# Dense stage between attention layers of a graph network, moved chunk by chunk into the attention pass

## What is computed

```python
def _gat_layer(x, src, dst, W, a_src, a_dst, b):
    h = (x @ W.T).reshape(N, H, C)
    alpha_s = jnp.einsum('nhc,hc->nh', h, a_src)
    alpha_d = jnp.einsum('nhc,hc->nh', h, a_dst)
    e = _leaky_relu(alpha_s[src] + alpha_d[dst])
    e_max = jax.ops.segment_max(e, dst, num_segments=N)
    e_exp = jnp.exp(e - e_max[dst])
    denom = jax.ops.segment_sum(e_exp, dst, num_segments=N)
    alpha = e_exp / denom[dst]
    msg = alpha[:, :, None] * h[src]
    out = jax.ops.segment_sum(msg, dst, num_segments=N)
    return out.reshape(N, H * C) + b
...
x = jax.nn.relu(_gat_layer(x, src, dst, W1, as1, ad1, b1))
x = jax.nn.relu(_gat_layer(x, src, dst, W3, as3, ad3, b3))
return _gat_layer(x, src, dst, W2, as2, ad2, b2)
```

## Time and profile before

| | us |
|---|---|
| median of 3 runs | 11625.31 (11618.93 to 11647.12) |
| the profiled execution | 11634.58 |
| its span | 11632.5 |
| attention passes: first gather, last gather starts | 5139.9, 11494.5 |
| first dense stage between passes (reciprocals from) | 7210.2 |
| second dense stage between passes (reciprocals from) | 9369.2 |

### The profile page before, as it was taken

The page is one execution under the profiler, slowest core; times in us unless marked ns, Lnnn a source line. Parts: engine busy times, 40 slices in busy tenths (PEclk is TensorE's granted clock), DMA queues, the critical chain, the costliest instruction groups (busy, mean ns, idle before and its releaser), DMA issues. The chain is left out here.

```text
span 11632.5 us, 269882 instructions
## 1 busy us (share of the span) xinstructions
PE 8371.0 (72%) x95122; PEld 6886.6 (59%) x95123; DVE 7236.0 (62%) x21427; ACT 2833.5 (24%) x9590; POOL 8097.8 (70%) x8039
## 2 busy tenths in 40 slices
PE   4878888889999799956666667566666666666665
PEld 3777777768778687835555555455555545555553
DVE  5777777779999654565555556555555565555556
ACT  2444333434444455520000001100000020000001
POOL 5777777737577475727777775677777757777774
PEclk9898888979999898955555555555555555555555
DMA  4666666649899686812222221222222212222221
GB/s 133 189 188 190 188 178 182 187 127 258 222 257 258 193 267 210 254 25 43 43 43 43 43 43 33 43 43 43 43 43 43 43 33 43 43 43 43 43 43 28
DMA packets 1192998, 1285.98 MB, mean 111 GB/s; under 512 B 234298, under 2 KB 1039893, under 8 KB 1191410
## 3 DMA queue, kind: packets, MB, share of 16 engines
q1 hardware_dynamic: 629602, 628.36, 17.7%
q0 software_dynamic: 254464, 283.59, 12.8%
q10 hardware_dynamic: 307600, 356.66, 10.6%
HBM read 982.93 MB, written 284.81 MB: 109 GB/s over the span
## 5 line engine op out<-in xcount | busy, mean ns | idle before, releaser
L2285 POOL DMA_INDIRECT rows<-gat_table,wgt x2457 | 2353.5, 958 | 962.2 <-issue 747.9
L2285 POOL DMA_INDIRECT Y<-gat_table,wgt x2394 | 2293.6, 958 | 729.6 <-issue 729.6
L2466 DVE TENSOR_TENSOR rep<-rep,layers 128x560 f32<-128x560 f32 x693 | 514.9, 743 | 2372.6 <-ACT rep L2399 2372.6
L1001 POOL DMA_INDIRECT bins<-scratch,slots x1288 | 1373.2, 1066 | 500.0 <-issue 384.9
L2311 PE MATMUL bank<-rep,work 128*32 128x80 f32 x11088 | 527.7, 341 | 1495.5 <-DVE rep L2466 1495.5
L2311 PEld LDWEIGHTS bank<-rep,work 128*32 128x32 f32 x11088 | 324.0, 158 | 1836.6 <-DVE rep L2466 1836.6
L2358 PE MATMUL bank<-work,msg 128*72 128x32 f32 x9702 | 1308.7, 309 | 0.0
L2358 PEld LDWEIGHTS bank<-work,msg 128*72 128x72 f32 x9702 | 1215.8, 237 | 44.5
L1191 DVE TENSOR_TENSOR xT<-counts,xT 112x480 f32<-112x480 f32 x1716 | 1114.5, 650 | 80.0 <-issue 48.3
L1069 PE MATMUL bank<-xT 112*64 112x120 f32 (+1 forms) x13728 | 1138.5, 277 | 26.4 <-ACT xT L1379 24.4
L2345 PE MATMUL bank<-scratch,work 128*128 128x64 f32 x2772 | 754.8, 426 | 515.5 <-DVE scratch L2436 515.5
(11 more groups left out here) (277 smaller groups left out, 16940.1 us busy)
## 6 DMA issues: line engine op xcount, KB each, us to landing
xT<-bins ACTq DMA_DIRECT2D x1716, 119.0 KB
work<-adj SPq DMA_DIRECT2D x184, 780.0 KB
work<-near_table SPq DMA_DIRECT2D x1118, 128.0 KB
near_table<-work SPq DMA_DIRECT2D x598, 128.0 KB
xT<-near_table SPq DMA_DIRECT2D x598, 128.0 KB
adj<-work ACTq DMA_DIRECT2D x299, 240.0 KB
bins<-zeros ACTq DMA_DIRECT2D x46, 1547.0 KB, 9.6
work<-in_attr SPq DMA_DIRECT2D x231, 224.0 KB
```

The costliest lines, as they stand in the source:

```text
L1001: nc.gpsimd.indirect_dma_start(bins, bass.IndirectOffsetOnAxis(slots[b % RANK_LEAD][:, r * G + j:r * G + j + 1], 0), binf[r][:, j, :], Non ...
L2285: nc.gpsimd.indirect_dma_start(rows[g % GR][:, j, :], None, gat_table, bass.IndirectOffsetOnAxis(edge_sources[:, g * G + j:g * G + j + 1], ...
```

## The change

The dense stages behind the first and the second pass go; their steps become part of `gat_pass`. Chunk c is due when turn `EARLY[c]` + 7 has added the last group that can reach its columns, by the mean number of edges of a node and two groups to spare (21, 40, 59 and so on; the last two are 229 and 231). Its steps then follow one to a turn, in eight turns: denominators on PE, reciprocal and product on DVE, activation on ACT, forward on PE, copies on DVE and ACT, the store on SP. One chunk has one set of banks (0, 1 and 2) and of buffers. A chunk is now 512 adjacent columns. Rows go to a second table, since the pass still gathers from the first; the tables take turns. DVE, not POOL, sets the denominators' rows back to 1. The set-up finds, for each chunk, the lowest destination of all groups from `EARLY[c]` on; where one still points into the chunk, `widest` is raised, and the fallback, which has a dense stage of its own, takes over. (Its part of the diff is left out.)

```diff
@@ -52,6 +52,8 @@
+MARGIN = 2
+EARLY = [-(-CH * (c + 1) * E // (N * GE)) + MARGIN for c in range(NCH - 1)] + [NG]
@@ -131,7 +133,7 @@
-        gat_table = dram("gat_table", (NP, ROW))
+        gat_tables = [dram(f"gat_table{i}", (NP, ROW)) for i in range(2)]
@@ -408,6 +410,13 @@
+                lowest_left, late = [qbuf[:].rearrange("p t d -> p (t d)")[:, NG + i * (NCH - 1):NG + (i + 1) * (NCH - 1)] for i in range(2)]
+                for c in range(NCH - 1):
+                    link(nc.vector.tensor_reduce(lowest_left[:, c:c + 1], first[:, EARLY[c]:], AX, ALU.min))
+                link(nc.vector.scalar_tensor_tensor(late, counts[:, 1:NCH], float(CH), lowest_left, ALU.mult, ALU.is_gt))
+                link(nc.vector.tensor_reduce(bad[:, 1:2], late, AX, ALU.max))
+                link(nc.vector.tensor_scalar(bad[:, 1:2], bad[:, 1:2], float(WIN), None, ALU.mult))
+                link(nc.vector.tensor_tensor(widest[:], widest[:], bad[:, 1:2], ALU.max))
@@ -2246,12 +2310,20 @@
-        def gat_pass(name):
+        def gat_pass(k, nxt, gat_table, next_table):
...
+            DELAY = 7
+            STEPS = 8
+            bias = col["gb" + k]
+            def chunk_at(n, step):
+                c = EARLY.index(n - DELAY - step) if n - DELAY - step in EARLY else None
+                return c if nxt else None
@@ -2272,8 +2344,17 @@
-                    for g in range(NG):
-                        body(g)
+                    def keep(c):
+                        sp.wait_ge(q["gtile_ready"].handle, q["gtile_ready"].at(c + 1))
+                        sp.dma_start(next_table[columns(c), :].rearrange("(p t) d -> p t d", t=TC), gbuf).then_inc(s_gtab[0].handle, 16)
+                    for n in range(NG + DELAY + STEPS + 2):
+                        if real(n):
+                            body(n)
+                        if chunk_at(n, STEPS) is not None:
+                            keep(chunk_at(n, STEPS))
+                    if nxt:
+                        sp.wait_ge(s_gtab[0].handle, s_gtab[0].at(16 * NCH))
@@ -2358,6 +2439,25 @@
+                    def denominators(c):
+                        pe.wait_ge(q["acc_done"].handle, q["acc_done"].at(EARLY[c]))
+                        if due(c):
+                            pe.wait_ge(q["inverted"].handle, q["inverted"].at(c))
+                        nc.tensor.matmul(bank[0][LO, :], denom[:], accT[0:ROW, columns(c)], start=True, stop=True).then_inc(q["prod_ready"].handle, 1)
+                    def forward(c):
+                        pe.wait_ge(q["x_ready"].handle, q["x_ready"].at(c + 1))
+                        if due(c):
+                            pe.wait_ge(q["gtile_ready"].handle, q["gtile_ready"].at(c))
+                            pe.wait_ge(q["kept"].handle, q["kept"].at(c))
+                        nc.tensor.matmul(bank[1][0:D + 40, :], attend[nxt][:], x_of, start=True, stop=True)
+                        for t in range(TC):
+                            last = nc.tensor.matmul(bank[2][:, t * ROW:(t + 1) * ROW], x_of.rearrange("r (p t) -> r t p", t=TC)[:, t, :],
+                                                    attend[nxt][:, 0:ROW], start=True, stop=True)
+                        last.then_inc(q["nodes_ready"].handle, 1)
@@ -2370,9 +2470,13 @@
+                        if chunk_at(n, 4) is not None:
+                            forward(chunk_at(n, 4))
+                        if chunk_at(n, 0) is not None:
+                            denominators(chunk_at(n, 0))
...
-                    for n in range(NG + 6):
+                    for n in range(NG + DELAY + STEPS):
@@ -2400,6 +2504,19 @@
+                    def activate(c):
+                        ac.wait_ge(q["mean_ready"].handle, q["mean_ready"].at(c + 1))
+                        if due(c):
+                            ac.wait_ge(q["nodes_ready"].handle, q["nodes_ready"].at(c))
+                        nc.scalar.activation(x_of, mean_of, ACT.Relu, bias=bias).then_inc(q["x_ready"].handle, 1)
+                    def keep_scores(c):
+                        ac.wait_ge(q["nodes_ready"].handle, q["nodes_ready"].at(c + 1))
+                        nc.scalar.activation(xT[0:H, columns(c)], bank[1][D:D + H, :], ACT.Copy)
+                        nc.scalar.activation(auxT[0:H, columns(c)], bank[1][D + 32:D + 32 + H, :], ACT.Copy).then_inc(q["kept"].handle, 1)
@@ -2407,8 +2524,12 @@
-                    for n in range(NG + 5):
+                        if chunk_at(n, 5) is not None:
+                            keep_scores(chunk_at(n, 5))
+                        if chunk_at(n, 3) is not None:
+                            activate(chunk_at(n, 3))
+                    for n in range(NG + DELAY + STEPS):
@@ -2520,7 +2641,28 @@
-                    DELAY = 7
+                    def invert(c):
+                        ve.wait_ge(q["prod_ready"].handle, q["prod_ready"].at(c + 1))
+                        if due(c):
+                            ve.wait_ge(q["mean_ready"].handle, q["mean_ready"].at(c))
+                        nc.vector.reciprocal(inverse_of, bank[0][LO, :]).then_inc(q["inverted"].handle, 1)
+                    def mean(c):
+                        ve.wait_ge(q["inverted"].handle, q["inverted"].at(c + 1))
+                        if due(c):
+                            ve.wait_ge(q["x_ready"].handle, q["x_ready"].at(c))
+                        nc.vector.tensor_tensor(mean_of, inverse_of, accT[LO, columns(c)], ALU.mult).then_inc(q["mean_ready"].handle, 1)
+                        nc.vector.memset(accT[D:ROW, columns(c)], 1.0).then_inc(q["cleared"].handle, 1)
+                    def take(c):
+                        ve.wait_ge(q["nodes_ready"].handle, q["nodes_ready"].at(c + 1))
+                        if due(c):
+                            ve.wait_ge(s_gtab[0].handle, s_gtab[0].at(16 * c))
+                        nc.vector.tensor_copy(accT[LO, columns(c)], bank[1][LO, :])
+                        nc.vector.tensor_copy(gbuf, by_tile(bank[2], ROW)).then_inc(q["gtile_ready"].handle, 1)
@@ -2540,6 +2682,12 @@
+                        if chunk_at(n, 5) is not None:
+                            take(chunk_at(n, 5))
+                        if chunk_at(n, 2) is not None:
+                            mean(chunk_at(n, 2))
+                        if chunk_at(n, 1) is not None:
+                            invert(chunk_at(n, 1))
@@ -2562,7 +2710,11 @@
-            gat_further(name)
+            if nxt:
+                s_gtab[0].done(16 * NCH)
+                for n in ["prod_ready", "inverted", "mean_ready", "cleared", "x_ready", "nodes_ready", "kept", "gtile_ready"]:
+                    q[n].done(NCH)
+            gat_further(k, nxt, gat_table, next_table)
@@ -2574,11 +2726,9 @@
-        gat_pass("gat0")
-        gat_dense("1", "3")
-        gat_pass("gat1")
-        gat_dense("3", "2")
-        gat_pass("gat2")
+        gat_pass("1", "3", *gat_tables)
+        gat_pass("3", "2", *gat_tables[::-1])
+        gat_pass("2", None, gat_tables[0], None)
```

More of the change, by code:

```diff
@@ L530, in further @@
                             closing(g)
+                if ending is not None:
+                    ending()
                 engine.nop()
@@ L628, in _, with gat_further @@
                     further(ve, group, window, closing, NG, cleared)
-        def gat_further(name):
+        mean_of, inverse_of, x_of = [scratch[0:D, i * CH:(i + 1) * CH] for i in range(3)]
+        columns = lambda c: slice(c * CH, (c + 1) * CH)
+        def gat_further(k, nxt, gat_table, next_table):
+            ending = lambda body: body if nxt else None
             with nc.Block() as block:
@@ L646, in group, with dense @@
                                      ).then_inc(f_load.handle, 16)
-                    further(sp, group, whole=NG, opening=restored)
+                    def dense():
+                        for c in range(NCH):
+                            sp.wait_ge(f_restored.handle, NCH + 2 + c)
+                            sp.dma_start(next_table[columns(c), :].rearrange("(p t) d -> p t d", t=TC), gbufs[0]).then_inc(f_load.handle, 16)
+                        sp.wait_ge(f_load.handle, 16 * (2 * NCH + 2 * NG))
+                    further(sp, group, whole=NG, opening=restored, ending=ending(dense))
                 @block.gpsimd
@@ L697, in window, with dense @@
                         last.then_inc(token_tensor_vector.handle, 1)
-                    further(pe, group, window, whole=NG, opening=restored)
+                    further(pe, group, window, whole=NG, opening=restored, ending=ending(dense))
                 @block.scalar
                 def _(ac):
+                    def dense():
+                        for c in range(NCH):
+                            ac.wait_ge(token_vector_scalar.handle, 1)
+                            ac.sem_clear(token_vector_scalar.handle)
+                            nc.scalar.activation(x_of, mean_of, ACT.Relu, bias=col["gb" + k]).then_inc(token_scalar_tensor.handle, 1)
                     def group(g, base=0.0):
```

(2 more changed lines are left out.)

42 lines of the change are left out of this document (36 added, 6 removed).

## The result

The changed kernel takes **11532.94 us** (median of 4 runs, 11528.61 to 11535.81) against 11629.9 for the kernel before (4 runs, 11618.93 to 11647.12): a ratio of 0.9915, with an interval of 0.9898 to 0.9932. It is 0.85% faster, with an interval that leaves 1 out. It lies inside the stated range, outside the 11488 to 11522 that the forecast itself was given, and 33 us above the 11500 forecast. The two profiled executions have spans of 11532.9 and 11632.5, so 99.6 us went where 125.6 were forecast.

The account below looks back on a forecast made before the run. POOL's gathers and their issue were taken to bound the passes. Boundaries -132, set-up +4.4 and gathers beside DVE +2 summed to -125.6 us: 11509 from the profiled 11634.6, or 11500 against the runs' median; range 11484 to 11535.

Parts of the forecast that it names:

- What bounds the kernel: Attention passes: POOL's seven gathers and their issue, 8.83 us a group; at each pass boundary POOL gathers nothing for 89 us.
- the first rival: Pass boundaries: chunks 11 and 12 run one behind the other at strided prices, 37 us a boundary, 11528 us; chance 0.07.
- The chain behind T0: Pass boundary: steps of chunks 11 and 12 from the last add's end to the next first gather, 23 us for 89.
- its strided rival: Dense steps of a chunk: DVE's product or copy at the price with a stride, 1.22 us, against 0.62 over adjacent columns.
- The check block that now stands here as well: ... 1.5: Pass boundary: the check block takes 1.9 us as before, less what is counted already, so it adds 1.5 us.
- Set-up +4.4: Set-up: 12 more reductions and four small operations on DVE's chain add 4.4 us (3 to 6).
- One body in nineteen runs some 2 us late. That delays no gather: First two passes: PE's chunk work exceeds one body's slack; gathers have about 53 us before POOL would wait.
- I take +2 us, because the 0.94 row is nearest in kind: First two passes: gathers beside a busier DVE cost 2 us in all, between bounds of nothing and 63 us.
- 14 us from the chunks' own products: First two passes: by the skill's rule alone, each chunk's 0.62 us product is lost 22 times; about 11512 us.
- The other rivals: Passes: DVE stretches gathers (0.06), DVE shuts POOL out (0.06), or each pass goes through the fallback, over 17,600 us (0.01).
- gathers stretched by every added instruction: First two passes: each of 110 added DVE instructions lengthens a gather by 0.57 us, 63 us in all, 11561 us; chance 0.06.
- POOL shut out: First two passes: POOL stands during every added DVE instruction and following gathers stretch, 186 us, about 11684 us; chance 0.06.

Follow-up runs that it names:

- the short-fallback run: The changed kernel with the fallback's own dense stage left out, nothing else; 11521.61 us.
- the added product: The kernel before, with one more DVE product of 64 x 512 in each turn, both inputs in SBUF, result not used; 11756.35 us.
- the copy: The kernel before, with one more DVE copy of 64 x 512 from PSUM in each turn, result not used; 11745.34 us.
- the six-chunk fallback: The changed kernel with the fallback's dense stage written out for 6 chunks in place of 13; 11529.22 us.

## Why the prediction was right, and where it was off

- **The range: right in part by luck.** What bounds the kernel, and what the change wins, were right. But the forecast's own band, 11488 to 11522, was missed; the range reached to 11535 to take in the first rival, whose time (11528) came nearest and whose mechanism did not happen. 11532.94 lies in the room made for it.
- **What bounds the kernel: right.** POOL's gathers and their issue set the pace in a pass, and POOL's idle 89 us at a boundary was the thing to win. It shrank to 25.1 at both.
- **The chain behind T0: nearly right in its steps and in size.** The first reciprocal began at T0 + 1.2 (forecast 1.6), chunk 12's at 6.6 (7.2), ACT ended chunk 12's activation at 12.1 (13.3), and the last copy ended at 17.4 (18.3). The adjacent-column price taken from another line, 0.62, measured 0.68 (the row at 7228.38); its strided rival was 1.22. PE's forward is used at 3.9, though its rows add up to 4.06; it took 3.8. One wait was another: the forward of chunk 12 waited last for DVE's row copy of chunk 11, which ended at 7236.26 behind chunk 12's product and memset, 0.3 after ACT's activation, which the prediction had as the last. The two chunks overlapped, so the first rival (37 us a boundary) is out.
- **"The check block that now stands here as well: ... 1.5": mis-sized.** From the copies' end to the gather it took 7.8 and not 4.3. The step carried over the old check block's time, when the body it jumps over had grown. From the start of PE's branch to the gather it took 4.9 (7244.1 to 7248.96); in the short-fallback run it takes 1.5 (7226.4 to 7227.87), just as forecast, so this is the term: PE's branch waits there for instructions.
- **Set-up +4.4: right**, 4.37 by its rows. The +8.1 to the first gather is not all from the change.
- **"One body in nineteen runs some 2 us late. That delays no gather": right as it was meant, wrong as a sum.** No gather waited for a message; POOL's only wait is its issue. But late bodies put DVE's operations at other moments, and that is where most of the 17.4 us come from.
- **"I take +2 us, because the 0.94 row is nearest in kind": the step that failed.** In the earlier trace rows the product L2466 begins 0.34 us after the gather at 7313.73, past the instant, 0.12 after the start, at which the held gathers find theirs. The row beneath, 0.97, was the telling one: the tensor-scalar runs from 7314.73 to 7315.14 across the start at 7314.98, and 7315.14 + 0.82 is where the gather ends. The row chosen could not decide the question. The term also counted only the added instructions as able to hold a gather, 110 of them; the holding was done by those already there.
- **The Trainium skill's rule (SBUF — State Buffer, Who interferes with whom)**, that a DVE instruction with two SBUF inputs contends with a GpSimd instruction that reads SBUF: the prediction said that the trace did not bear it out. That reading was wrong. The 199 gathers under the added product against the 195 under the copy bear out which kind of instruction holds one. What the prediction made of it, 14 us from the chunks' own products, is not what happened either: they cost 0.8 us.
- **The other rivals.** Gathers at a mean of 0.963 and 0.964 in the first two passes (1556.50 and 1559.44 us over 1617), waiting for their issue alone, are a little past the 0.95 to 0.96 that the prediction named for itself, and rule out gathers stretched by every added instruction (0.98 and over) and POOL shut out. The fallback was never taken: 4851 gathers, as before.

Of the 26 us between forecast and trace, the passes make 16.7, the boundaries 4.2, and the stretch ahead of the first gather 3.7; the last is not told apart from the spread of traces, and 1.5 is in pass 3 and the end.

No version was found that beats the changed kernel with its fallback whole. The run without the fallback's dense stage shows what a shorter one could be worth, about 6.6 us; a dense stage written as a loop was not tried.

## What to carry to other kernels

When work moves beside an engine that sets the pace, price what the move does to the moments at which the work already there meets it, and not only the added instructions: here an added operation that could not touch a gather cost 30 us a pass by shifting one that could. A row shows that two operations don't collide only if they overlap at the instant that matters; compare several pairs at different offsets before taking a price of nothing. And count code that is jumped over: a fallback that never runs can cost microseconds at each place where it is passed.

## What the runs showed of the hardware that was not expected

- Every gather of over 1.0 us had a DVE operation with both inputs in SBUF, or a tensor-scalar with int32 input, running 0.12 us after its start, and ended 0.82 after an operation of these kinds; where such an operation was 0.3 us or more into its row at that instant, 512 of 512 and 489 of 489 gathers were held to its end. 65 gathers under a reciprocal out of PSUM of 3.34 us and 195 under a copy out of PSUM of 0.68 us were not held.
- A branch over unexecuted code behind a pass took PE 0.34 to 0.46 us or 2.88 to 3.85 us, and nothing between; the kernel with the six-chunk fallback has one of each, at two places with the same instructions to jump over. A 16 KB packet of instructions landed inside each of the 16 long ones and none of the 25 short ones.
- Spreading a long DVE operation over four turns did not lower the gathers' loss, it spread it.
